# Reordering the queues of three engines in the spectral-attention stage of a two-expert-layer block

## The reference

```python
x = x + 0.5 * ffn(layernorm(x))
x = x + attn(layernorm(x))
x = x + 0.5 * ffn(layernorm(x))

def attn(x):                      # x: 8 x 1024 x 256
    q, k, v = x @ Wq.T, x @ Wk.T, x @ Wv.T
    fk = rfft(k); fk = fk / (abs(fk) + EPS)
    fq = rfft(q); fq = fq / (abs(fq) + EPS)
    fv = rfft(v)
    fkv = cumsum(fk * fv, axis=tokens)
    return x + irfft(fkv * conj(fq))
```

## Time and profile before

| | |
|---|---|
| median of 3 runs | 1603.56 us (1603.27 to 1604.35) |
| the profiled execution | 1603.56 us, its span 1601.5 us |
| PE, PEld, DVE, ACT, POOL busy over the span | 89%, 80%, 80%, 59%, 49% |
| mean granted TensorE clock | 0.975 of full |
| attention stage | about 655 to 970 us of the span |

### The profile page before, as it was taken

The page is one execution under the profiler, slowest core; times in us unless marked ns, Lnnn a source line. Parts: engine busy times, 40 slices in busy tenths (PEclk is TensorE's granted clock), DMA queues, the critical chain, the costliest instruction groups (busy, mean ns, idle before and its releaser), DMA issues.

```text
span 1601.5 us, 34763 instructions
## 1 busy us (share of the span) xinstructions
PE 1420.4 (89%) x9656; PEld 1275.3 (80%) x9657; DVE 1280.0 (80%) x3425; ACT 942.1 (59%) x1435; POOL 790.1 (49%) x992
## 2 busy tenths in 40 slices
PE   0899999998999998899998877999999998999994
PEld 0677777776999998788887765777777787999994
DVE  4688888876789998578789976888888876799996
ACT  4344333332877776799998883434333335888883
POOL 0344554443576766533444433444554433767664
PEclk9999999998999999999999987999999999999997
DMA  8511111114578776100001010111111125688887
GB/s 287 165 50 51 54 54 48 50 44 129 150 214 231 228 235 183 56 1 1 0 0 53 27 40 28 38 48 51 54 54 51 47 70 153 183 250 273 268 273 229
DMA packets 108284, 177.01 MB, mean 111 GB/s; under 512 B 13936, under 2 KB 73208, under 8 KB 107896
## 3 DMA queue, kind: packets, MB, share of 16 engines
q1 hardware_dynamic: 82280, 104.16, 23.0%
q0 software_dynamic: 25920, 71.86, 12.0%
HBM read 95.75 MB, written 86.70 MB: 114 GB/s over the span
## 4 chain that ended last, share of the span: by engine, by line
PE 28%; DVE 21%; issue 20%; DMA 10%; ACT 8%; POOL 8%; DVEq 3%; SPq 1%; ACTq 1%; POOLq 0%
PE bank L722 7%; PE bank L724 7%; PE bank L723 7%; DMA lists<-a_rows,a_slots 7%; POOL lists L438 6%; DVE b_yb L1269 2%; ACT a_rows L556 2%; PE bank L871 2%; DVE a_gate_u L1132 2%; DVEq L1249 2%; DVE X L1281 2%; DVE X L1344 1%; DMA b_xb<-lists 1%; PE bank L959 1%; PE bank L961 1%
## 5 line engine op out<-in xcount | busy, mean ns | idle before, releaser
L450 POOL DMA_INDIRECT results<-b_yb,b_goal x284 | 327.0, 1151 | 192.4 <-issue 103.5
L438 POOL DMA_INDIRECT lists<-a_rows,a_slots x256 | 256.7, 1003 | 148.2 <-POOL a_rows L431 53.0
L507 ACT ACTIVATE a_uh<-a_gate_u 128x512 fp32r<-128x512 f32 x128 | 77.1, 625 | 228.2 <-PE bank L724 195.3
L722 PE MATMUL bank<-a_sw2h,a_uh 128*128 128x256 f32 x512 | 153.7, 300 | 55.0 <-DVE a_xtl L1005 42.4
L722 PE MATMUL bank<-b_xbth,b_w1h 128*128 128x256 f32 x568 | 171.5, 302 | 0.0
L722 PE MATMUL bank<-ew_h,b_hth 128*128 x568 | 160.2, 282 | 0.0
L724 PE MATMUL bank<-b_xbth,b_w1l 128*128 128x256 f32 x568 | 160.2, 282 | 0.0
L723 PE MATMUL bank<-b_xbtl,b_w1h 128*128 128x256 f32 x568 | 160.0, 282 | 0.0
L724 PE MATMUL bank<-ew_h,b_htl 128*128 x568 | 158.9, 280 | 0.0
L723 PE MATMUL bank<-ew_l,b_hth 128*128 x568 | 158.8, 279 | 0.0
L525 ACT ACTIVATE a_gate_u<-bank 128x512 f32<-128x512 f32 x128 | 76.0, 593 | 126.4 <-DVE a_ul L1005 79.0
(11 more groups left out here) (214 smaller groups left out, 4775.0 us busy)
## 6 DMA issues: line engine op xcount, KB each, us to landing
b_xb<-lists SPq DMA_DIRECT2D x142, 264.0 KB
b_yt<-results SPq DMA_DIRECT2D x112, 256.0 KB
X<-in_L_attn_x SPq DMA_DIRECT2D x16, 512.0 KB, 4.4
out<-X SPq DMA_DIRECT2D x16, 512.0 KB
results<-b_yb,b_goal POOLq DMA_INDIRECT x284
lists<-in_c_fill SPq DMA_DIRECT2D x16, 264.0 KB, 3.9
w_raw_ew<-in_L_ffn_ew SPq DMA_DIRECT2D x2, 2048.0 KB, 13.8
lists<-a_rows,a_slots POOLq DMA_INDIRECT x256, 2.4
```

The source lines that it names most:

```text
L438: pool.indirect_dma_start(out=lists, out_offset=bass.IndirectOffsetOnAxis(ap=slots[:, q, k, j:j + 1], axis=0), in_=rows[:, q, j, :], in_of ...
L450: pool.indirect_dma_start(out=results, out_offset=bass.IndirectOffsetOnAxis(ap=goal[:, u, blk:blk + 1], axis=0), in_=YB[:, u % 4, blk, :], ...
L507: return act.activation(o, i, ACT.Copy)
L722: pe.matmul(o, a("h"), b("h"), start=first, stop=False)
```

## The change

No instruction is added or taken away. Three engines get another order within the step.

- ACT: the V copy of chunk s-2 moves from behind the square of K to behind the first logarithm. The copy to FK now follows the square.
- PE: the XN transposes of chunk s+1 move from behind the prefix matmuls to ahead of them.
- DVE: the residual add of chunk s-2 moves from ahead of L1390 in step s to the beginning of step s+1, ahead of L1334. The low half of XA moves from the middle of the prefix product to ahead of it. The adds of the last two chunks come in the calls for steps 17 and 18.

```diff
--- before.py
+++ after.py
@@ -639,11 +639,6 @@
                 if now:
                     act.wait_ge(s_kps, s + 1)
                     act.activation(SQ[:, 0:J], kq_ps, ACT.Square).then_inc(s_ksq, 1)
-                if inside(s - 2, CH):
-                    act.wait_ge(s_ptp, s - 1)
-                    atleast(act, s_aps, s * 2 - 4)
-                    copy(VT[:], bank[:, 0:2, :]).then_inc(s_ph, 1)
-                if now:
                     atleast(act, s_kvd, s)
                     copy(FK[:], kq_ps).then_inc(s_kev, 1)
                 if now or prev:
@@ -654,6 +649,10 @@
                         act.wait_ge(s_qsum, s)
                         atleast(act, s_p, s - 1)
                     ca.link(act.activation(inverse, power, ACT.Ln, bias=tiny[:, 0:1]))
+                if inside(s - 2, CH):
+                    act.wait_ge(s_ptp, s - 1)
+                    atleast(act, s_aps, s * 2 - 4)
+                    copy(VT[:], bank[:, 0:2, :]).then_inc(s_ph, 1)
                 if now or prev:
                     ca.settle()
                     ca.link(act.activation(inverse, inverse, ACT.Exp, scale=0.5))
@@ -948,6 +947,10 @@
                     if isinstance(s, int) and s == 0:
                         pe.wait_ge(s_mlo, 6)
                     spectrum(2, 2).then_inc(s_qps, 1)
+                if nxt:
+                    pe.wait_ge(s_txn, s + 2)
+                    atleast(pe, s_ph, s - 1)
+                    transposed(XN_FIRST[1] if isinstance(s, int) and s == 0 else XN)
                 if prev:
                     pe.wait_ge(s_kvd, s)
                     pe.wait_ge(s_px, s)
@@ -960,10 +963,6 @@
                         if before[j] is not None:
                             ins = pe.matmul(o, ones_f, before[j], start=False, stop=True)
                     ins.then_inc(s_cps, 1)
-                if nxt:
-                    pe.wait_ge(s_txn, s + 2)
-                    atleast(pe, s_ph, s - 1)
-                    transposed(XN_FIRST[1] if isinstance(s, int) and s == 0 else XN)
                 if old:
                     if isinstance(s, int) and s == 2:
                         pe.wait_ge(s_inv, 16)
@@ -1312,21 +1311,18 @@
             def attention(s, par, half, meanwhile=None):
                 prev, now, nxt, far = inside(s - 1, CH), inside(s, CH), inside(s + 1, CH), inside(s + 2, CH)
                 lo, hi = slice(1, NF), slice(NF + 1, D)
-
-                def attended(c, at):
-                    dve.wait_ge(s_txn, c + 1)
+                if inside(s - 3, CH):
+                    at = 0 if isinstance(s, int) and s == CH + 2 else 4
+                    dve.wait_ge(s_txn, s - 2)
                     for h in range(2):
-                        dve.wait_ge(s_aps, c * 2 + (h + 1))
+                        dve.wait_ge(s_aps, s * 2 + (h - 5))
                         apart(dve)
                         for i in range(2):
-                            t = c * J + (2 * h + i)
+                            t = s * J + (2 * h + i - 3 * J)
                             xt = X[:, bass.ds(t, 1), :].rearrange("p a d -> p (a d)")
                             ins = dve.scalar_tensor_tensor(xt, xt, rstd_1[:, bass.ds(t, 1)],
                                                            bank[:, at + h, i * D:(i + 1) * D], ALU.mult, ALU.add)
                         ins.then_inc(s_aout, 1)
-
-                if isinstance(s, int) and s == CH + 2:
-                    attended(CH - 1, 0)
                 if prev:
                     dve.wait_ge(s_root, s)
                     atleast(dve, s_cps, s - 1)
@@ -1365,6 +1361,9 @@
                     ch.link(dve.tensor_tensor(FK[:, :, lo], FK[:, :, lo], FK[:, :, hi], ALU.subtract))
                     ch.settle()
                     ch.link(dve.tensor_tensor(FK[:, :, hi], TA[:], TB[:], ALU.add))
+                if nxt:
+                    dve.wait_ge(s_ah, s + 2)
+                    low(XA["l"][:], bank[:, 0:2, :], XA["h"][:]).then_inc(s_al, 1)
                 if prev:
                     c_ps, fq = bank[:, 6:8, :].rearrange("p b (j d) -> p (b j) d", j=2), FQ[:, 1 - par]
                     ch.settle()
@@ -1374,17 +1373,10 @@
                     ch.link(dve.tensor_tensor(TB[:], c_ps[:, :, hi], fq[:, :, lo], ALU.mult))
                     ch.settle()
                     dve.tensor_tensor(fq, c_ps, fq, ALU.mult).then_inc(s_cused, 1)
-                if nxt:
-                    dve.wait_ge(s_ah, s + 2)
-                    low(XA["l"][:], bank[:, 0:2, :], XA["h"][:]).then_inc(s_al, 1)
-                if prev:
                     dve.wait_ge(s_cused, s)
                     ch.link(dve.tensor_tensor(fq[:, :, lo], fq[:, :, lo], fq[:, :, hi], ALU.add))
                     ch.settle()
                     ch.link(dve.tensor_tensor(fq[:, :, hi], TB[:], TA[:], ALU.subtract))
-                if inside(s - 2, CH) and (prev or not isinstance(s, int)):
-                    attended(s - 2, 4)
-                if prev:
                     ch.settle()
                     dve.wait_ge(s_root, s + 1)
                     ch.link(dve.tensor_tensor(fq[:, :, 0:NF + 1], fq[:, :, 0:NF + 1], RB[:, J:], ALU.mult))
@@ -1417,6 +1409,7 @@
                 return step
 
             step_a = attention(CH, 0, CH // 2, next_layer)
+            attention(CH + 1, 1, CH // 2)
             step_a(-2, 0, -1)
             step_a(-1, 1, -1)
             attention(CH + 2, 0, CH // 2 + 1)
```

## The result

The changed kernel takes 1613.1 us (median of 4 runs, 1612.8 to 1613.9) against 1603.4 for the kernel before (4 runs): ratio 1.006, 95% interval 1.0043 to 1.0078, 9.7 us slower. Forecast were 14.8 us more and 1618.4.

What follows compares the result with a forecast made beforehand. A loop across engines, none full, was taken to set the step. Terms -1.96+11.8-0.3+3.1+2.2 gave +14.8 us on 1603.56, so 1618.4 us, range 1606 to 1623.

Steps and rivals of the forecast that it cites:

- The forecast step, 5.18+14.82: Spectral-attention step: 5.18 us from mark (start of L1390) to FK's copy, 14.82 to next mark; 20.00 against 18.32.
- POOL in the way: POOL's sum of squares (L469) starts 2.75 us behind the mark, on L1334; L1335 is then held, costing 1.09 us.
- my rival: "POOL misses the gap": L1335 is not lengthened, step 18.92 us, total 1606.3 to 1610.4, middle 1608; chance 0.18.
- Steps 1 and 2: First steps of the stage, no add ahead: 0.77 us earlier, then 17.35 against 18.54; together -1.96 us.
- Seven steps: Seven steps between marks 703.57 and 831.80: each 20.00 us against 18.32, together +11.8 us.
- Gather steps: Four steps with the gather-add (L1344), DVE full: 82.5 us against 82.78, -0.3; bounds 4 x 19.9 to 4 x 21.0.
- Last two steps: Steps 14 and 15 of the stage: 19.5 and 18.9 us, together 38.4 against 35.3, +3.1.
- Behind the stage: Last prefix +1.57 us through POOL's chain, next stage's first transposes +0.6 for chunk 14's add; +2.2 in all.
- By this edit alone ACT's own queue would be the bound (17.39): PE's transposes ahead of the prefix end ACT's 0.71 us wait, leaving ACT's queue period of 17.39 us as step.
- the rival "faster": FK's copy is not held, ACT's queue bounds the step at 17.39 us, total about 1596; chance 0.12.
- Table load behind a logarithm: ACT's V copy there: no load taken; as a rival, extra loads of 1.28 us, 1628 to 1638; chance 0.05.
- What would show it: Signs: steps near 20.0, ACT idle 1.5 to 2.6 us before FK's copy, L1335 at 1.77, PE's wait before L940.

Runs made afterwards that it cites:

- act_back_pool: Changed kernel with ACT's V copy back behind the square of K and POOL's sum of squares waiting for KV: 1602.9 us, ratio 0.9993.
- act_back: Changed kernel with only ACT's V copy put back behind the square of K: 1606.5 us, ratio 1.0010 to the kernel before.
- after_again: The changed kernel run and profiled once more with no edit: 1614.1 us, ratio 1.0069 to the kernel before.
- act_only: Kernel before with ACT's edit alone, the V copy moved behind the first logarithm: 1603.7 us, ratio 0.9994.
- late_adds: Changed kernel, V copy back behind the square; residual add behind KV from step 10; POOL's sum held for KV in earlier steps: 1597.9 us, ratio 0.9960.
- add_back: Changed kernel with the residual add back ahead of the mark, low half of XA left where the change puts it: 1608.2 us, ratio 1.0026.
- kv_first_act: kv_first with ACT's V copy put back behind the square of K: 1599.8 us, ratio 0.9974 to the kernel before.
- pe_only: Kernel before with PE's edit alone, XN transposes ahead of the prefix matmuls: 1607.9 us, ratio 1.0027.
- pe_act: Kernel before with PE's and ACT's edits and none on DVE: 1608.3 us, ratio 1.0022.
- kv_first: Changed kernel with KV formed ahead of the residual add, and one wait of PE's inverse transform made explicit: 1601.7 us, ratio 0.9987.
- add_only: Kernel before with one edit alone, the residual add moved from ahead of the mark to ahead of KV: 1610.7 us, ratio 1.0053.
- pool_waits: Changed kernel with POOL's sum of the squares of K also waiting until DVE has formed KV: 1609.4 us, ratio 1.0037.

## Why the prediction was right, and where its steps were off

The direction and the mechanism were right. The add ahead of KV delays the copy to FK, whose cover ACT's edit takes away at the same time. Where the step of 19.93 comes from can now be laid out: 18.05 with neither (act_back_pool), 0.98 for POOL on the first KV instruction (act_back, 19.03), 0.90 for the V copy out of the cover. The forecast was 20.00.

- **The forecast step, 5.18+14.82.** In the trace L1331 ends 5.04 behind the mark, the copy to FK starts 0.04 later, and 14.86 lie from there to the next mark. So the one part was 0.10 too long and the other 0.04 too short.
- **POOL in the way: right in size, wrong in its rule and in its victim.** I had POOL break in at the gap ahead of L1335 (now L1331), and that one stand still. It was the first of the two, L1330, that stood still, at 1.67 to 1.68 in all of seven steps. I had read the rule from the earlier trace rows as one thing; over all kernels of this study the rows say something else. Where POOL's sum starts 0.15 to 0.17 us ahead of the first KV instruction, DVE is held until the sum ends (21 of 21 times: seven steps each of the changed kernel, after_again and act_back). Where it starts from 0.07 ahead of it to 0.42 behind it, both KV instructions go through at 0.68 and POOL waits for both, for 2.0 to 2.5 us in all (57 of 59 times). From 0.51 to 0.82 behind it the same holds 10 of 11 times, with a shorter wait of POOL., on which I built, are one of the three exceptions; the others are the same step of act_only and step 14 of late_adds, where the second KV instruction took 1.76 and 1.74. The Trainium skill (SBUF — State Buffer, Who interferes with whom) has it that the first to issue keeps the port for its whole instruction and the other stands; for the first KV instruction the trace agrees with it where POOL starts 0.15 ahead or more, and with the page I would have had the right victim; at 0.03 to 0.07 ahead (add_back) POOL's record starts first and DVE is not held all the same. That POOL, once it waits, doesn't get in between the two back-to-back instructions, the section doesn't say, and why the three exceptions differ is open.
- **The size came out by luck.** The sum placed POOL at 2.75 behind the mark, 0.03 ahead of L1330. By the rows of add_back, where it starts 0.03 to 0.04 ahead of the first KV instruction and that one passes at 0.69, this would have been a miss of POOL, and the step the 18.92 of my rival. It came at 2.63, because the mark lies 0.34 behind the root and not 0.20. So one tenth of a microsecond decides 1 us a step. That rival I gave 0.18, with its threshold put at 3.07; by the rows it lies between 2.63 and 2.71 behind the mark, on the other side of my 2.75.
- **Steps 1 and 2: -1.96 forecast, -0.97 measured** (marks 684.46 and 702.60 against the earlier trace rows). The place of the first mark wanders by a microsecond between executions of one kernel (in after_again mark 2 lies at 703.73, 0.16 behind the kernel before), so this gain is not clear of scatter; the length of step 2 is. The second step is 18.14 instead of 17.35: the copy to FQ waits 0.40 us for PE, and the prefix product starts 1.36 behind L1004 and not 1.13. kv_first_act did this step in 17.34.
- **Seven steps: +11.8 forecast, +10.3 measured.** Step 3 is only 18.96, because POOL came 0.57 behind L1330 there and held nobody up; the six others are 19.93.
- **Gather steps: -0.3 forecast, -2.2 measured, the mis-sized term.** L1330 takes 0.79 to 0.90 in them, where I had added 0.57. DVE is full there and the mark lies behind the root, so POOL's sum starts 1.77 behind the mark and is nearly over when L1330 comes, which I had not followed through. The 80.5 us lie near my lower bound of 4 x 19.9.
- **Last two steps: +3.1 forecast, +1.7 measured** (36.99 against 35.30). Step 14 is 19.16 and step 15 17.83; the latter I had at 18.9 with POOL's full overlap, which did not come.
- **Behind the stage: +2.2 forecast, +3.6 measured.** Mark 15 is 8.81 later. POOL's chain starts 10.39 later than in the earlier trace rows, 1.58 more, as forecast (1.57). The last prefix takes 6.15 us instead of 5.48, +0.67, for which I had no term (the clock, below). The first transposes of the next stage (L746, 981.42 against 969.03) are 12.39 later, another 1.33: the whole of the add of chunk 14 behind L1391, of which I had hidden half. At the table cast at the end of the routing it is 12.7 (1328.64 before, 1341.37 and 1341.36 in the two profiles of the changed kernel). The medians say 9.7 and 10.2 with intervals that reach to 12.5 and 13.5. I carried all of the stage's loss to the end; how much of 12.7 the last stage gives back isn't settled.
- **"By this edit alone ACT's own queue would be the bound (17.39)" was wrong**, and with it the size of the rival "faster". pe_only and pe_act show 18.90 and a time 0.2 to 0.3% over before. Had FK's copy not been held, the result would not have been 1596; with KV ahead of the add and the copy to FK free, kv_first takes 1601.7 and, with ACT's old order, 1599.8, and that by the gather steps. What I missed is that the chain through the prefix was only the 0.24 of the earlier trace rows shorter than the one I followed.
- **Table load behind a logarithm:** it did not come; four loads in a step, as before. The Trainium skill (ScalarE: Activation LUTs, Table sets) was right in this.
- **What would show it:** the ACT wait ahead of FK's copy (2.54, forecast 1.5 to 2.6), none ahead of the XA high copy, the DVE wait ahead of the low part, and PE's wait ahead of L939 (0.80 and 1.31 by turns) came. L1331 at 1.77 did not.

What the edits cost. Put singly into the kernel before: PE's +0.27%, ACT's -0.06% (no difference), the move of the add +0.53%. PE's and ACT's with the low half of XA (add_back) cost +0.26%, the whole change +0.69%. Taken back from the changed kernel, the move of the add gives 0.43%, 7 us, and ACT's edit 0.59%. The price of an edit depends on which loop the others have left the longest: the prefix loop in pe_only, by its waits the one through the V spectrum in add_only, the one through the copy to FK in the changed kernel. The low half of XA alone and the changed kernel without PE's edit were not run.

## What to carry to other kernels

Before an edit shortens one loop across engines, look for the next longest: the idle time in brackets at the meeting point of two chains (0.24 us here) is all that an edit of the one chain can win, and an instruction that is put into the other chain costs from there on. An instruction ahead of one that waits may be the cover of that wait: moved away it costs its own length, although the same move in an order without the wait costs nothing. Where two engines meet on SBUF operands, a tenth of a microsecond in who starts first can be worth a microsecond a step; put an instruction with a PSUM operand beside the other engine's, as kv_first and late_adds do.

## What the runs showed of the hardware

- A POOL addition and a DVE product with both inputs in SBUF exclude each other. With POOL's recorded start 0.15 to 0.17 us ahead DVE's 0.69 becomes 1.67 (21 times); from 0.07 ahead to 0.42 behind POOL's 1.27 becomes 2.0 to 2.5 (57 of 59). The residual add, with one input in PSUM, and POOL's sum run side by side at full speed (1.65 and 1.27).
- A POOL instruction that waits is passed by a second DVE instruction that follows the first at 0.6 us, and not only by the first. For the three exceptions (DVE 1.74 to 1.77 and POOL 1.29 to 1.59, all in steps 14 and 15) I have no explanation.
- A table load was held 0.41 us for the operand of the activation behind it, that is, for POOL's sum (pool_waits). In this program the load didn't run ahead of the wait that stands in front of its activation. Whether it could isn't shown.
- TensorE's clock at the end of the stage. The windows of the changed kernel (busy time of each engine, then the granted clock):

```profile
962.00:968.00 6.00, 0.01 (x1) 0.01 (x1) 5.86 (x9) 5.93 (x7) 4.93 (x3) 0.50 0.00 0
968.00:973.00 5.00, 4.97 (x12) 4.01 (x13) 1.77 (x8) 3.15 (x5) 1.61 (x4) 0.50 0.00 0
973.00:981.00 8.00, 4.80 (x22) 3.84 (x20) 6.42 (x11) 1.20 (x3) 0.00 (x0) 0.93 0.00 0
981.00:984.00 3.00, 1.94 (x8) 1.57 (x8) 2.01 (x9) 0.61 (x1) 0.49 (x3) 0.50 0.00 0
```

PE did nothing from 962 to 968 and had the lower of its two levels (0.50 is 1.2 GHz of 2.4). It kept it through the first 5 us of the last prefix, whose pairs of matmuls took 1.06 us and later 0.59. The kernel before had the lower level there too, for a shorter time:

```profile
956.00:961.00 5.00, 3.36 (x8) 2.77 (x9) 3.28 (x12) 4.92 (x6) 2.64 (x4) 0.50 0.00 0
```

In all the last prefix took 6.15 us against 5.48, and this 0.67 is part of the 12.4. In the changed kernel, after another 3.6 us of idle time, ahead of 981.42, it fell again, and the first eight transposes of the next stage took 1.94 us. In the kernel before the same eight took 1.07 at a clock of 0.97. The forecast had no term for either. The slower transposes lie behind the start of L746, at which the 12.4 us are read; between there and the table cast the difference grew by 0.3 us only.
